# Writing the context part of a cross-attention and FFN kernel out tile by tile, with its side loads in pieces

## The chip, the cores and the metric

The kernel runs on one core of a Trainium2 chip. The metric is the device time of one execution in microseconds (us). Three runs of the kernel before took 1319.31 to 1321.22 us, median 1320.01.

## The reference

The inputs are x (64 x 512 x 512), a context (64 x 77 x 512) and the weights of one attention layer and one FFN layer, all float32. Cut to what matters:

```python
qh = rope(einsum('bse,ehd->bshd', layernorm(x), Wq))   # 16 query heads, 4 key/value heads, 32 wide
kh = rope(einsum('bse,ehd->bshd', ctx, Wk)); vh = einsum('bse,ehd->bshd', ctx, Wv)
attn = softmax(qh @ kh^T / sqrt(32))
x = x + mean_over_heads(attn @ vh) @ Wo
w_scale = mean(abs(weight))
q_weight = sign(weight) * (abs(weight) > 0.5 * w_scale)          # ternary weight
i_scale = max(abs(layernorm(x))) / 127
x = x + (clip(round(layernorm(x) / i_scale)) @ q_weight^T) * w_scale * i_scale + bias
```

## The kernel before, in words

There are three parts. The **context part** turns the 64 x 77 = 4928 context rows into keys and values and writes them to two scratch tensors in HBM, `k_scr` and `v_scr`. Then the attention part goes over 128 pairs of x tiles in a pipeline of seven stages, and last the FFN part goes over the 64 batches. The change touches the context part and the SyncE instructions right behind it; it lies in about the first 120 of 1318 us.

The context part works in 39 tiles of 128 rows (the last has 64), numbered 0 to 38. No scheduler decides anything: each engine has its own instruction list, written by hand, and semaphores join them. Five engines work on a tile:

- SyncE issues nearly all DMAs, in the order of its list. For tile j it loads the context rows of tile j+4 (`ctx_load`, L324) into one of four buffers, stores the keys of tile j-2 and the values of tile j (`kv_store`, L330 and L331; in the last tiles L365 and L371). Each store waits for the data, and what stands behind it on SyncE waits with it.
- TensorE multiplies tile j (`ctx_kv`, L1065, 12 matmuls), transposes the rows of tile j+2 (`ctx_T`, L1054), which waits for the load of that tile, and transposes the keys of tile j-2 (`ctx_kT`, L1073).
- ScalarE copies the transposed rows (L572), the keys and values out of PSUM (L582, L585) and the transposed keys (L595).
- VectorE makes the low parts of the transposed rows for tile j+1 (L753), two small steps on the values of tile j (L776, L781), and the low part of the keys of tile j-2 (L787). Behind these four it does weight preparation in some tiles.
- GpSimd does the rotary embedding of the keys (L478, L484).

The first tiles and the last are written out; the ones between run in a hardware loop of four tiles a turn (on GpSimd two). The weight preparation on VectorE stands in these places: the sum of the four query groups of Wq in tiles 5 to 7 (L801 to L805), the sum of absolute FFN weights in tile 8 (L809), the bias rows in tiles 9 to 12 (L813 to L829), the centring of Wq and the thresholds at tile 32 (L850 to L857), and the ternary FFN weight in tiles 33 to 36, three instructions a tile (L860 to L864). The Wq weight, the FFN weight and the first x batch are loaded with 1 MB each behind tiles 0, 2 and 3 (L344, L347, L351), the second and third x batch near the end (L362), the fourth behind the first keys. The two rotary tables `kcos` and `ksin` (624 KB each) are loaded before the first tile. The first keys and values of the attention part come back from scratch (`kv_step`, L400 and L404, ten DMAs a batch) when all stores have landed.

Of the kernel before, what the change touches and what calls it, by code (L numbers as in the profile page):

```python
# [90 lines left out]
def build(nc, x, ctx_in, wq, wk, wv, wo, fw, fb, ident_d, qcos_d, qsin_d, kcos_d, ksin_d, out):  # L91
# [11 lines left out]
    with stack:  # L103
# [204 lines left out]
        def _(sp):  # L308
            sp.dma_start(ctx_sb[:, 0, :], ctx_rows[0:P, :]).then_inc(c_in[0], 16)
            sp.dma_start(ident[:, :], ident_d).then_inc(ident_in, 16)  # L310
            sp.dma_start(wkv[:, :, 0, :], wk.rearrange("(c p) n -> p c n", p=P)).then_inc(wkv_in, 16)
            sp.dma_start(wkv[:, :, 1, :], wv.rearrange("(c p) n -> p c n", p=P)).then_inc(wkv_in, 16)
            sp.dma_start(ctx_sb[:, 1, :], ctx_rows[P:2 * P, :]).then_inc(c_in[1], 16)
            for n in range(4):
                sp.dma_start(wo4[D * n:D * n + D, :], wo).then_inc(wo_in, 16)
            for n in range(2, 4):
                sp.dma_start(ctx_sb[:, n, :], ctx_rows[P * n:P * n + P, :]).then_inc(c_in[n], 16)
            sp.dma_start(kcos, kcos_d).then_inc(ktable_in, 16)
            sp.dma_start(ksin, ksin_d).then_inc(ktable_in, 16)
# [13 lines left out]

            sp.wait_ge(zeroed, ZEROED)
            for n in range(4):
                ctx_load(n, n)
                if n < 2:
                    sp.wait_ge(v_copied, n + 1)
                    sp.wait_ge(v_ready, n + 1)
                    sp.dma_start(v_scr[n * P:n * P + P, :, :], v_sb[:, n, :, :]).then_inc(v_out[n], 16)  # L340
                else:
                    kv_store(n, n)
                if n == 0:
                    sp.dma_start(wq_sb.rearrange("p c h g d -> p c (h g d)"),  # L344
                                 wq.rearrange("(c p) h g d -> p c (h g d)", p=P)).then_inc(wq_in, 16)
                elif n == 2:
                    sp.dma_start(fw_sb, fw.rearrange("(c p) k -> p c k", p=P)).then_inc(fw_in, 16)  # L347
                    sp.dma_start(qcos[:, :, :], qcos_d).then_inc(qtable_in, 16)
                    sp.dma_start(qsin[:, :, :], qsin_d).then_inc(qtable_in, 16)
                    sp.dma_start(fbias, fb.unsqueeze(0).broadcast_to([BR, E])).then_inc(fb_in, 16)  # L350
            sp.dma_start(x_sb[:, 0, :, :], xv[0]).then_inc(x_in[0], 16)  # L351
            groups = (CT - 4) // 4
            with sp.Fori(1, groups) as g:
                for n in range(4):
                    ctx_load(g * 4 + n, n)
                    kv_store(g * 4 + n, n)
            for j in range(groups * 4, CT + 3):
# [951 lines left out]
```

## Time and profile before

| what | value |
|---|---|
| profiled execution, its span | 1319.5 us, 1317.7 us |
| TensorE matmul, weight load busy | 1267.9 us (96%), 1085.9 us (82%) |
| VectorE, ScalarE, GpSimd busy | 1181.8 us (90%), 1025.1 us (78%), 791.2 us (60%) |
| mean granted TensorE clock | 0.990 of full speed |
| DMA of a context tile | rows in 256 KB, keys out 128 KB, values out 68 KB |
| Wq load, 1024 KB, issued at 15.16 us | 5.7 us to landing |
| `kcos` and `ksin` loads, 624 KB each | 6.1 and 7.1 us to landing |
| main chain of waits, whole execution | VectorE 47%, TensorE 31%, issue 15% |

How to read it: the shares of busy time are averages over all three parts and say little about the context part, which is a tenth of the span. The timeline, cut to one engine, shows each group of instructions with its start, its length and, in brackets, how long the engine was idle before it and what ended that. Times below count from the start of the span. Buffers that lie in the large x and x1 arrays, such as the context rows, the keys and values before they are stored and the FFN weight, all appear under the name `x_sb` in the trace.

### The profile page before, as it was taken

Reading aid. Unit: us, or ns where it says so; the run is one execution under the profiler, and the core shown is the slowest. Engines: PE = TensorE matmul, PEld = TensorE weight load, DVE = VectorE, ACT = ScalarE, POOL = GpSimd, SP = SyncE. Lnnn points to the kernel's source line nnn. Section 1 sums busy time; section 2 is a strip of 40 time slices with the busy share of each in tenths; the row PEclk is TensorE's granted clock in tenths of the full one; section 3 lists DMA queues with packets and bytes.
Section 4 is the critical chain, followed back from the end, with each engine's and each line's share of the span. In section 5 each row is a group of like instructions: output and inputs, shape, how many; then the busy total and the mean of one; then the engine's idle time right before and its main releaser. Section 6 shows DMA issues by size and latency. Waiting matters only on the chain.

```text
span 1317.7 us, 36811 instructions
## 1 busy us (share of the span) xinstructions
PE 1267.9 (96%) x9848; PEld 1085.9 (82%) x9911; DVE 1181.8 (90%) x2772; ACT 1025.1 (78%) x2338; POOL 791.2 (60%) x1536
## 2 busy tenths in 40 slices
PE   5897999999999999999999999999969999999998
PEld 5796999999999999999999999999935555555554
DVE  4876899999999999999999999999978888888887
ACT  3454788888888888888888888888857878888886
POOL 3564888888888888888888888888820000000000
PEclk9999999999999999999999999999979999999999
DMA  8574355555555555555546452323108999999945
GB/s 266 166 216 133 107 158 182 154 183 161 176 165 171 165 171 167 170 171 166 178 159 187 150 169 76 102 80 98 37 5 332 400 401 395 401 399 404 406 201 223
DMA packets 100815, 265.18 MB, mean 201 GB/s; under 512 B 49705, under 2 KB 65769, under 8 KB 72114
## 3 DMA queue, kind: packets, MB, share of 16 engines
q1 hardware_dynamic: 100786, 264.86, 58.8%
q8 instruction: 10, 0.16, 0.1%
q14 instruction: 19, 0.16, 0.0%
HBM read 139.64 MB, written 125.17 MB: 201 GB/s over the span
## 4 chain that ended last, share of the span: by engine, by line
DVE 47%; PE 31%; issue 15%; DMA 2%; DVEq 2%; SPq 1%; ACT 1%; POOL 1%; POOLq 0%; ACTq 0%
PE bank L1248 18%; DVE amax L898 10%; DVE x_sb L930 8%; DVE e_sb L944 6%; DVE mx_sb L940 5%; DVE bn_sb L889 5%; PE bank L1239 4%; PE bank L1246 3%; DVE qT_sb L912 2%; PE bank L1065 2%; DVE rinv_sb L886 2%; DVE ve_sb L918 2%; DVE bn_sb L881 2%; DVE mv_sb L904 1%; DMA x_sb<-in_ctx 1%
## 5 line engine op out<-in xcount | busy, mean ns | idle before, releaser
L1248 PE MATMUL bank<-wT,x_sb 128*128 128x512 f16 x1024 | 263.9, 380 | 3.5 <-issue 0.2
L1168 PE MATMUL bank<-wqs,xT_sb 128*128 128x128 f32 x2048 | 259.7, 280 | 0.2
L718 ACT ACTIVATE x_sb<-bank,mean,cols 128x512 f32<-128x512 f32 x256 | 196.0, 774 | 67.6 <-PE bank L1248 67.3
L1168 PEld LDWEIGHTS bank<-wqs,xT_sb 128*128 128x128 f32 x2048 | 238.2, 191 | 7.1 <-ACT xT_sb L640 0.8
L1216 PE MATMUL bank<-v_blk,pT_sb 103*128 103x136 f32 x1536 | 199.0, 279 | 0.3 <-ACT pT_sb L682 0.3
L1216 PEld LDWEIGHTS bank<-v_blk,pT_sb 103*128 103x128 f32 x1536 | 190.6, 190 | 0.5 <-ACT pT_sb L682 0.5
L1248 PEld LDWEIGHTS bank<-wT,x_sb 128*128 128x128 f16 x1024 | 100.5, 98 | 106.8 <-issue 1.6
L930 DVE SCALAR_TENSOR_TENSOR x_sb<-x_sb,negm,bank 128x512 f32 (+1 forms) x256 | 179.5, 742 | 7.9 <-PE bank L1179 2.7
L898 DVE TENSOR_REDUCE amax<-x_sb (+1 forms) x128 | 156.0, 1218 | 23.2 <-DVE bn_sb L889 8.0
L691 ACT ACTIVATE sq_sb<-x_sb 128x512 bf16 (+1 forms) x256 | 161.4, 631 | 18.7 <-DVE x_sb L930 1.4
L1005 DVE TENSOR_TENSOR x_sb<-x_sb 128x512 f32 (+1 forms) x256 | 164.5, 683 | 1.2 <-ACT x_sb L718 1.2
L682 ACT ACTIVATE pT_sb<-bank 103x384 f32<-103x384 f32 x256 | 111.7, 489 | 53.1 <-PE bank L1189 53.1
L640 ACT ACTIVATE xT_sb<-bank 128x512 f32<-128x512 f32 x256 | 138.9, 595 | 7.6 <-PE bank L1138 3.0
L1203 PE MATMUL bank<-k_blk,qT_sb 128*128 128x308 f32 x768 | 140.1, 317 | 1.8 <-DMA k_blk<-k_scr 1.8
L504 POOL TENSOR_TENSOR rs<-ve_sb,mhalf 128x2 f32 (+1 forms) x128 | 89.5, 700 | 79.9 <-DVE ve_sb L875 79.9
L1138 PE MATMUL bank<-ident,x_sb 128*128 128x128 f32 x1024 | 133.0, 273 | 0.0
L667 ACT ACTIVATE e_sb<-e_sb,rs_sb 128x308 f32<-128x308 f32 x256 | 129.2, 568 | 0.0
L997 DVE TENSOR_SCALAR x_sb<-bank 128x1024 f16<-128x1024 f16 x128 | 88.5, 691 | 44.6 <-PE bank L1239 43.0
L940 DVE TENSOR_REDUCE mx_sb<-bank 128x4 f32<-128x308 f32 x256 | 110.1, 471 | 11.0 <-PE bank L1203 8.1
L1138 PEld LDWEIGHTS bank<-ident,x_sb 128*128 128x128 f32 x1024 | 117.0, 141 | 0.0
L1203 PEld LDWEIGHTS bank<-k_blk,qT_sb 128*128 128x128 f32 x768 | 111.0, 189 | 2.2 <-DMA k_blk<-k_scr 2.0
L1189 PEld LDWEIGHTS bank<-ident,e_sb 128*103 128x103 f32 x768 | 98.5, 168 | 15.4 <-issue 1.3
(126 smaller groups left out, 2584.4 us busy)
## 6 DMA issues: line engine op xcount, KB each, us to landing
out_y<-x_sb SPq DMA_DIRECT2D x112, 1024.0 KB, 7.2
x_sb<-in_x SPq DMA_DIRECT2D x64, 1024.0 KB, 6.5
x_sb<-out_y SPq DMA_DIRECT2D x48, 1024.0 KB, 9.0
x_sb<-in_ctx SPq DMA_DIRECT2D x38, 256.0 KB, 2.8
k_blk<-k_scr SPq DMA_DIRECT2D x256, 19.2 KB, 5.5
k_scr<-x_sb SPq DMA_DIRECT2D x38, 128.0 KB, 2.3
v_scr<-x_sb SPq DMA_DIRECT2D x38, 68.0 KB, 2.3
v_blk<-v_scr SPq DMA_DIRECT2D x128, 10.2 KB
```

Of the source, the lines that this page charges most:

```text
L640: act.activation(xT_sb[:, t, :, :].rearrange("p c r -> p (c r)"), bank[t][:, :], ACT.Copy).then_inc(xT_copied_t, 1)
L691: act.activation(sq_sb[:, :], x1_at(kj, gj, t), ACT.Square, accum_out=ssq[:, bass.ds(2 * j + t, 1)]).then_inc(sq_done, 1)
L718: act.activation(u_sb[:, t, :], bank[4 + t][:, :], ACT.Identity, bias=stat_of(mean1, j, t, back), scale=cols[:, 6:7]).then_inc(scaled_t, 1)
L898: dve.tensor_reduce(amax[:, bass.ds(2 * j, 2)], x1_at(kj, gj).rearrange("p (t e) -> p t e", t=2), AX.X, ALU.max, apply_absolute_value=True ...
L930: dve.scalar_tensor_tensor(out=x1_at(kj, gj, t), in0=x_sb[:, kj // 2, 2 * (kj % 2) + t, :], scalar=negm[:, kj, t:t + 1], in1=bank[t][:, :] ...
L940: dve.tensor_reduce(mx_sb[:, t, :], bank[4 + t][:, 0:SC].rearrange("p (h a) -> p h a", h=HEADS), AX.X, ALU.max).then_inc(mx_ready, 1)
L1005: dve.tensor_tensor(x1_tile, x1_tile, u_sb[:, t, :], ALU.add).then_inc(sum_done_t, 1)
L1138: last = pe.transpose(bank[t][:, c * P:(c + 1) * P], x_sb[:, kj // 2, 2 * (kj % 2) + t, c * P:(c + 1) * P], ident[:, :])
L1168: last = pe.matmul(bank[2][:, t * HD:(t + 1) * HD], xT_sb[:, t, c, :], wqs[:, c, :], start=c == 0, stop=c == EC - 1)
L1203: last = pe.matmul(bank[4 + t][:, 0:SC], qT_sb[:, a, t * P:(t + 1) * P], k_blk[:, slot, b, :].bitcast(F32R), start=n == 0, stop=n == 2)
L1216: last = pe.matmul(bank[6][:, t * HEADS * VC:(t + 1) * HEADS * VC], pT_sb[0:CR, t, c * P:(c + 1) * P], v_blk[0:CR, slot, c, :, :].rearrang ...
L1248: last = pe.matmul(bank[4 + t][:, :], q16T_sb[:, t, c, :], wT[:, c, :], start=False, stop=c == EC - 1)
```

## The change

The hardware loops of the context part are gone on all engines: its 39 tiles are written out, and the side work is placed by tile number. The 1 MB loads of Wq and the FFN weight become four pieces of 256 KB each, behind tiles 3 to 6 and 8 to 11; the rotary tables come as their first 8 tiles' rows ahead and the rest (496 KB each) behind tiles 1 and 2; the four x batches are loaded behind tiles 16, 22, 28 and 34. The keys and values of batches 0 and 1 are fetched behind tiles 20 and 30 instead of after all stores. The loads of Wk, Wv and Wo are issued by ScalarE instead of SyncE. On VectorE the Wq sum moves to tiles 9 to 11, the absolute sum is cut into four (tiles 13 to 16), the Wq centring stands in tile 16, the bias rows in 17 to 20, the thresholds in 21, and the ternary weight takes tiles 22 to 33, one instruction each. SyncE's order in a tile is context load, key store, value store, and then the side load. The core of the diff:

```diff
+KFIRST = 8
+WQ_SUM, WQ_MEAN, WQ_CENTRE = 9, 14, 16
+FW_SUM, FW_MEAN, FW_CUT, FW_TERN = 13, 19, 21, 22
+BIAS_ROWS = 17
+FW_T = FW_TERN + 4
+KV_AHEAD = (20, 30)
...
-            groups = (CT - 4) // 4
-            with sp.Fori(1, groups) as g:
-                for n in range(4):
-                    ctx_load(g * 4 + n, n)
-                    kv_store(g * 4 + n, n)
...
+            for j in range(CT + 3):
+                if j + 4 <= CT:
+                    sp.wait_ge(cT_done, j + 1)
+                    sp.dma_start(ctx_sb[0:rows, j % 4, :], ctx_rows[(j + 4) * P:(j + 4) * P + rows, :])\
...
+                if j == 1:
+                    sp.dma_start(kcos[:, KFIRST:CT + 1, :], kcos_d[:, KFIRST:CT + 1, :]).then_inc(ktable_in, 16)
+                elif j == 2:
+                    sp.dma_start(ksin[:, KFIRST:CT + 1, :], ksin_d[:, KFIRST:CT + 1, :]).then_inc(ktable_in, 16)
+                elif 3 <= j < 3 + EC:
+                    sp.dma_start(wq_sb[:, j - 3, :, :, :].rearrange("p h g d -> p (h g d)"), wq_rows[:, j - 3, :])\
+                      .then_inc(wq_in, 16)
+                elif 8 <= j < 8 + EC:
+                    sp.dma_start(fw_sb[:, j - 8, :], fw_rows[:, j - 8, :]).then_inc(fw_in, 16)
+                elif j == 12:
+                    sp.dma_start(fbias, fb.unsqueeze(0).broadcast_to([BR, E])).then_inc(fb_in, 16)
+                    sp.dma_start(qcos[:, :, :], qcos_d).then_inc(qtable_in, 16)
+                    sp.dma_start(qsin[:, :, :], qsin_d).then_inc(qtable_in, 16)
+                elif j in (16, 22, 28, 34):
+                    x_load((j - 16) // 6)
+                elif j in KV_AHEAD:
+                    b = KV_AHEAD.index(j)
...
+                    kv_step(b, b)
...
-            kv_step(0, 0)
-            kv_step(1, 1)
-            batch_step(3, 3, 0, store=False)
...
+            act.dma_start(wkv[:, :, 0, :], wk.rearrange("(c p) n -> p c n", p=P)).then_inc(wkv_in, 16)
+            act.dma_start(wkv[:, :, 1, :], wv.rearrange("(c p) n -> p c n", p=P)).then_inc(wkv_in, 16)
+            for n in range(4):
+                act.dma_start(wo4[D * n:D * n + D, :], wo).then_inc(wo_in, 16)
...
+                if FW_SUM <= j < FW_SUM + EC:
+                    c = j - FW_SUM
+                    dve.wait_ge(fw_in, 16 * EC)
+                    then(dve.tensor_reduce(fsum4[:, c:c + 1], fw_sb[:, c, :], AX.X, ALU.add,
+                                           apply_absolute_value=True))
...
+                o, part = (j - FW_TERN) // 3, (j - FW_TERN) % 3
+                if 0 <= o < EC:
+                    if part == 0:
+                        then(dve.tensor_scalar(fpos[:, o, :], fw_sb[:, o, :], cols[:, 2:3], None, ALU.is_gt))
+                    elif part == 1:
+                        then(dve.tensor_scalar(fneg[:, o, :], fw_sb[:, o, :], cols[:, 3:4], None, ALU.is_lt))
+                    else:
+                        dve.tensor_tensor(w16[:, o, :], fpos[:, o, :], fneg[:, o, :], ALU.subtract).then_inc(f_tern, 1)
```

SyncE's list in the loop of the kernel before, two tiles of a turn and its end (`x_sb<-in_ctx` is a context load, ISA and REGISTER_ALU rows compute and wait):

```order
L324 DMA x_sb<-in_ctx 128x512
L330 ISA
L330 DMA v_scr<-x_sb 128x136
L331 REGISTER_ALU
L331 DMA k_scr<-x_sb 256x1x128
L324 ISA
L324 DMA x_sb<-in_ctx 128x512
L330 ISA
L330 DMA v_scr<-x_sb 128x136
L331 REGISTER_ALU
L331 DMA k_scr<-x_sb 256x1x128
L353 REGISTER_ALU
```

SyncE's list in the changed kernel around tile 20 (line numbers of the changed kernel):

```order
L343 DMA x_sb<-in_ctx 128x512
L348 DMA k_scr<-x_sb 256x1x128
L354 DMA v_scr<-x_sb 128x136
L328 DMA k_blk<-k_scr 32x2x77 x4
L332 DMA v_blk<-v_scr 77x34
L332 DMA v_blk<-v_scr 26x34
L332 DMA v_blk<-v_scr 51x34
L332 DMA v_blk<-v_scr 52x34
L332 DMA v_blk<-v_scr 25x34
L332 DMA v_blk<-v_scr 77x34
L343 DMA x_sb<-in_ctx 128x512
```

Before, only stores stood between two context loads; now ten loads of keys and values stand between the stores of tile 20 and the next context load.

VectorE's list in the kernel before, tile 33, where the ternary weight is made:

```order
L753 TENSOR_TENSOR cT_parts<-bank,cT_parts 128x512
L776 TENSOR_TENSOR x_sb<-x_sb,wbar 128x128
L781 TENSOR_REDUCE x_sb<-x_sb 128x4
L787 TENSOR_TENSOR x_sb<-bank,x_sb 128x128
L860 TENSOR_SCALAR x_sb<-x_sb,cols 128x512
L863 TENSOR_SCALAR x_sb<-x_sb,cols 128x512
L864 TENSOR_TENSOR x_sb<-x_sb 128x512
L753 TENSOR_TENSOR cT_parts<-bank,cT_parts 128x512
```

VectorE's list in the changed kernel, tiles 22 and 23 (L734 is the old L753, L830 and L832 the old L860 and L863):

```order
L734 TENSOR_TENSOR cT_parts<-bank,cT_parts 128x512
L757 TENSOR_TENSOR x_sb<-x_sb,wbar 128x128
L762 TENSOR_REDUCE x_sb<-x_sb 128x4
L768 TENSOR_TENSOR x_sb<-bank,x_sb 128x128
L830 TENSOR_SCALAR x_sb<-x_sb,cols 128x512
L734 TENSOR_TENSOR cT_parts<-bank,cT_parts 128x512
L757 TENSOR_TENSOR x_sb<-x_sb,wbar 128x128
L762 TENSOR_REDUCE x_sb<-x_sb 128x4
L768 TENSOR_TENSOR x_sb<-bank,x_sb 128x128
L832 TENSOR_SCALAR x_sb<-x_sb,cols 128x512
```

The three instructions of one quarter of the weight, which stood together in one tile, now stand in three tiles, one in each.

## Rows read from the trace of the kernel before

**Rows 1.** Busy us of each engine by stretch (x instructions), TensorE clock, DMA.
```profile
28.00:29.00 1.00, 0.00 (x0) 0.00 (x0) 0.00 (x0) 0.00 (x0) 0.00 (x0) 0.57 1.09 397
...
58.00:80.00 22.00, 21.21 (x172) 19.87 (x170) 16.00 (x41) 12.47 (x40) 14.03 (x31) 1.00 0.74 210
```

**Rows 2.** TensorE timeline, starts of tiles 1, 9, 10, 14, 15, 20, 31, 38.
```profile
14.28 1.77 PE L1065 MATMUL bank<-wkv_parts,cT_parts 128*128 128x256 f32 x12
...
39.70 1.70 PE L1065 MATMUL bank<-wkv_parts,cT_parts 128*128 128x256 f32 x12
...
43.36 1.70 PE L1065 MATMUL bank<-wkv_parts,cT_parts 128*128 128x256 f32 x12 [1.41 <-DVE cT_parts L753]
...
54.52 1.70 PE L1065 MATMUL bank<-wkv_parts,cT_parts 128*128 128x256 f32 x12 [0.86 <-DVE cT_parts L753]
...
56.52 1.67 PE L1065 MATMUL bank<-wkv_parts,cT_parts 128*128 128x256 f32 x12
...
67.76 1.70 PE L1065 MATMUL bank<-wkv_parts,cT_parts 128*128 128x256 f32 x12
...
91.53 1.68 PE L1065 MATMUL bank<-wkv_parts,cT_parts 128*128 128x256 f32 x12
...
111.91 1.57 PE L1065 MATMUL bank<-wkv_parts,cT_parts 128*64 128x256 f32 x12 [0.86 <-DVE cT_parts L753]
```

**Rows 3.** TensorE timeline, context transposes that waited, and two tiles.
```profile
21.52 0.66 PE L1054 MATMUL bank<-ident,x_sb 128*128 128x128 f32 x4 [1.63 <-DMA x_sb<-in_ctx]
...
29.95 1.11 PE L1054 MATMUL bank<-ident,x_sb 128*128 128x128 f32 x4 [4.25 <-DMA x_sb<-in_ctx]
...
30.92 2.91 PE L1065 MATMUL bank<-wkv_parts,cT_parts 128*128 128x256 f32 x12
...
34.63 1.83 PE L1065 MATMUL bank<-wkv_parts,cT_parts 128*128 128x256 f32 x12
...
91.00 0.66 PE L1054 MATMUL bank<-ident,x_sb 128*128 128x128 f32 x4
```

**Rows 4.** SyncE timeline: DMA issues.
```profile
15.64 0.50 SPq L324 DMA_DIRECT2D x_sb<-in_ctx  x1
...
88.18 0.35 SPq L324 DMA_DIRECT2D x_sb<-in_ctx  x1
...
99.63 0.43 SPq L362 DMA_DIRECT2D x_sb<-in_x  x1
...
120.45 2.61 SPq L400 DMA_DIRECT2D k_blk<-k_scr  x4
...
123.10 2.29 SPq L404 DMA_DIRECT2D v_blk<-v_scr  x6
```

**Rows 5.** Landing times of line 324 (context rows) and line 362 (x).
```profile
DMA to landing us min/median/max: 2.6/2.8/7.8
...
DMA to landing us min/median/max: 5.7/5.8/5.8
```

**Rows 6.** VectorE timeline: weight preparation, and one tile with no extra work.
```profile
35.61 0.94 DVE L803 TENSOR_TENSOR wqs<-wqs,x_sb 128x512 f32<-128x512 f32 x1
...
98.08 0.69 DVE L851 TENSOR_TENSOR wqs<-wqs,x_sb 128x512 f32<-128x512 f32 x1
...
99.12 0.69 DVE L753 TENSOR_TENSOR cT_parts<-bank,cT_parts 128x512 fp32r<-128x512 f32 x1
...
100.56 0.48 DVE L860 TENSOR_SCALAR x_sb<-x_sb,cols 128x512 f32<-128x512 f32 x1
```

**Rows 7.** Timeline of all engines where the context part hands over.
```profile
114.56 0.59 ACT L619 ACTIVATE wT<-bank 128x512 f16<-128x512 f16 x1
...
124.79 1.12 PE L1203 MATMUL bank<-k_blk,qT_sb 128*128 128x308 f32 x6 [1.78 <-DMA k_blk<-k_scr]
...
125.05 0.74 POOL L554 TENSOR_TENSOR qa_sb<-qa_sb,qb_sb 128x256 f32<-128x256 f32 x1
...
126.62 0.38 PE L1150 MATMUL bank<-ident,qa_sb 128*128 128x128 f32 x2
```

More of the change, by code:

```diff
@@ L206, in build @@
         fpos = early(EC, E)
+        fsum4 = early(EC)
         w16 = early(EC, E // 2).bitcast(F16)
@@ new lines, in x_load, with kv_step @@
+            def x_load(b):
+                sp.dma_start(x_sb[:, b, :, :], xv[b]).then_inc(x_in[b], 16)
+            def kv_step(b, k):
+                at_least(sp, sc_done_t, 4 * (b - 2) + 4)
+                for h in range(HEADS):
+                    sp.dma_start(k_blk[D * h:D * h + D, k % 2, :, CTX * h:CTX * h + CTX],
+                                 k_scr[D * h:D * h + D, :, bass.ds(b * CTX, CTX)]).then_inc(k_in[k % 2], 16)
+                at_least(sp, pv_done, 2 * (b - 2) + 2)
+                for c, r, n, h, a in SEGS:
+                    sp.dma_start(v_blk[r:r + n, k % 2, c, h, :], v_scr[bass.ds(b * CTX + a, n), h, :])\
+                      .then_inc(v_in[k % 2], 16)
@@ L372, in _ @@
                       .then_inc(v_out[j % 4], 16)
+                if j == 1:
[15 more added lines that the diff above has]
+                    b = KV_AHEAD.index(j)
+                    for m in range(2):
+                        sp.wait_ge(k_out[m], 16)
+                        sp.wait_ge(v_out[m], 16)
+                    kv_step(b, b)
             sp.wait_ge(k_out[0], 16 * (CT // 2 + 1))
@@ L488, in _ @@
             pool.wait_ge(ktable_in, 32)
-            ctx_step(0, 0)
-            ctx_step(1, 1)
-            with pool.Fori(1, CT // 2) as g:
-                for n in range(2):
-                    ctx_step(g * 2 + n, n)
-            for j in range(2 * (CT // 2), CT + 1):
+            for j in range(CT + 1):
+                if j == KFIRST:
+                    pool.wait_ge(ktable_in, 64)
                 ctx_step(j, j % 2, P if j < CT else CLAST)
@@ L791, in _ @@
             wq_sum = wqs[:, :, :].rearrange("p c (h d) -> p (c h) d", h=HEADS)
-            for j in range(CHEAD):
-                if j >= 1:
-                    low_ctx(j + 1, (j + 1) % 2)
-                ctx_step(j, j % 4, j // 4)
-                if j >= 2:
+            for j in range(CT + 3):
+                if 1 <= j < CT:
+                    low_ctx(j + 1, (j + 1) % 2, P if j + 1 < CT else CLAST)
+                if j <= CT:
+                    ctx_step(j, j % 4, j // 4, P if j < CT else CLAST)
+                if 0 <= j - 2 < CT:
@@ L1077, in _ @@
             ctx_T(1, 1, 0)
-            for j in range(4):
+            for j in range(CT + 3):
                 if j == 0:
```

184 lines of the change are left out of this document (51 added, 133 removed).

## The prediction

> **What bounds the kernel now.** I read the busy time by stretch first. The change lies in the context part, which ends near 118 us. Everything behind it is the same instructions in the same order, so a gain or loss in the context part reaches the end of the kernel at full size. While 22 us of the old loop run, TensorE is busy 21.21 of them, VectorE 16.00, and the DMA engines' share is 0.74 at 210 GB/s [rows 1]. So the part is close to TensorE's pace where nothing disturbs it, but only just.
>
> Second, the timeline of TensorE. Call "step n" the time from the start of tile n's key and value matmuls (L1065) to the next tile's. Step 14 took 54.52 to 56.52: 2.00 us, TensorE never idle. The starts of steps 1, 9, 15, 20, 31 and 38 are 14.28, 39.70, 56.52, 67.76, 91.53 and 111.91 [rows 2]. That makes five stretches: A (8 steps) 25.42 us, B (6) 16.82, C (5) 11.24, D (11) 23.77, E (7) 20.38. At 2.00 a step they would need 74.0 of their 97.6 us. Three things make up the difference.
>
> (1) In A, TensorE waits for context rows: 1.63 us before 21.52 and 4.25 us before 29.95. Behind the second wait the clock is down: transposes take 1.11 us where 0.66 is usual, and step 6 takes 3.71 us (30.92 to 34.63) [rows 3]; the granted clock was 0.57 in 28 to 29 us, on its way to the 1.2 GHz level, with TensorE idle since 25.7 [rows 1]. Cold work cost 3.71-2.00, and 0.5 on the transposes: 2.2 us.
>
> (2) In B and E, VectorE's weight preparation stands between tiles. Its own four instructions a tile take 1.44 us (99.12 to 100.56) [rows 6], so 0.56 us a step are free. Step 9, with the 2048-wide absolute sum, took 3.66 us; steps 10 to 13 with the bias rows took 11.16 [rows 2].
>
> (3) In the loop the context load comes just in time: issued at 88.18, transposes of that tile at 91.00, as it lands (median landing 2.8) [rows 3, 4, 5]. SyncE issues it behind the two stores of an earlier tile, so its lead over the transposes is three steps minus the key/value chain. I put the slack at 0.2 us, an estimate: it is 0 in this row, a load issued just behind the loop's branch, and the whole loop loses only 0.16 a step against 2.00 (D, below), so the three loads of a turn without the branch before them have little more or less than their due. Anything issued ahead of a context load beyond that is TensorE idle time.
>
> **The change, part by part.** A base step in straight-line code: I take 2.05, between step 14's 2.00 and D's mean of 23.77/11 = 2.16.
>
> *Head loads in pieces (A).* The 1 MB loads of Wq, the FFN weight and x leave A; two table rests of 496 KB and four 256 KB pieces come in. At 397 GB/s [rows 1] 496 KB take 1.25 us, and one more issue costs 0.43 (99.63) [rows 4]. Ahead of a context load that is 0.43 + (1.25-0.43) - 0.2 = 1.05 late. A lateness in consecutive steps is paid once for two steps, because a step made longer gives the next load its lead; early loads also have about 0.3 more. Tables: 0.8. Pieces: 0.43 + 0.2 - 0.2 = 0.4 to 0.45, four of them, paid twice: 0.9. A = 16.4+0.8+0.9 = 18.1: **-7.3**. From both sides: -8 (no lateness) to -3 (a wait like the 1.63 and a cold restart stay).
>
> The skill page "DMA: Bandwidth & Descriptors" (Trainium skill, section Bandwidth) speaks against pieces: batch to 1 MiB or more. Here a 256 KB context load lands in 2.8 us and a 1 MB x load in 5.8, so by that rule four pieces one behind the other would hold the queue 4 x 2.8 - 5.8 = 5.4 us longer per weight, and A would gain 2 instead of 7. I don't take it: nothing waits between pieces, so their fixed part overlaps.
>
> *Weight and Wo loads issued by ScalarE.* They still land before the first matmuls, which hang on a chain of conversions behind them. I take 0; bounds: one issue earlier each, -0.9, to ScalarE being later, +0.4. The Trainium skill (same page, section Issuing engines are not separate DMA queues) says issuing from several engines saves only issue time; by it this is 0 to -0.9. No run here shows it.
>
> *FFN and Wq pieces and sums (B).* Four FFN pieces (2 x 0.45) overlap the three Wq sums, each up to 0.94 us (35.61) [rows 6] against 0.56 free: together 1.1. The absolute sum becomes four quarters of the one that cost step 9 1.6 us; they fit in the free 0.56 but for 0.1 each. The Wq mean's eight matmuls now stand in step 14: 0.9. B = 12.3+1.1+0.1+0.9 = 14.4: **-2.4**. The bias rows leave B for C and D.
>
> *C.* Three small loads behind tile 12: 3 x 0.43, of which step 14's 0.9 covers most: 0.4. Step 16 has the last quarter, its sum and the Wq centring (0.69 at 98.08 and its factor) [rows 6]: 1.2 over. First bias step 0.44, quarters 0.3. The x load behind tile 16 stands ahead of a context load. A context load issued at 15.64, right behind the 1 MB of Wq, was waited for until 21.52 [rows 3, 4]: 5.9 us, 3.1 more than 2.8. Late by 3.1+0.43-0.2 = 3.3, less the 1.4 by which steps 17 and 18 are longer: 2.0; I take 1.3, since an x load has 8 KB rows and 1 MB at 397 GB/s is 2.6 us. C = 10.25+1.2+0.44+0.3+0.4+1.3 = 13.9: **+2.7**.
>
> *D.* The other bias steps [rows 2]: 11.16 - 4 x 2.05 = 2.96, less what fell in C and under the x stall: 1.83. Transposes of the FFN weight, two groups at 0.25 each (an estimate; four small f16 transposes each): 0.5. The ternary steps, one instruction a tile, fit in 0.56 free. Then the early keys: behind tile 20 SyncE issues four key and six value loads, 2.61+2.29 = 4.9 us [rows 4], while the next context load and all stores wait behind it. Late by 4.9-0.2, less 1.1 of longer steps: 3.6 us idle in step 23. That is nearer to the 4.25 that let the clock fall than to the 1.63 that didn't: +2.2. The x load behind tile 22 comes within two steps of it and finds its lateness paid by the stall and the cold work. D = 22.55+1.83+0.5+3.6+2.2 = 30.7: **+6.9**.
>
> *E.* Before, the ternary work made a step 2.9 us (20.38/7; less VectorE's own 1.44 it is 1.5 a tile). Now 14.35 + 0.5 transposes. The x load behind tile 28 hits step 31 and the ten key loads behind tile 30 hit step 33; the second finds the first's stall in its lead, so both together cost about 4.9-0.2 = 4.65 (2 to 7 with a cold clock). E = 19.5: **-0.9**.
>
> *The seam.* The first score matmuls waited 1.78 us for the first keys (124.79) [rows 7]; those lie there now. But the next transposes (126.62) need GpSimd's result, which ends at 125.79, so 0.8 of it is gained. The last ternary copy on ScalarE (0.59 at 114.56) and its wait no longer stand before the x transposes' copies: 1.0. Together **-1.8** (0 to -3). The fourth x load leaves SyncE there: nothing waits for it.
>
> **Sum.** -7.3-2.4+2.7+6.9-0.9-1.8 = -2.8 us. The profiled execution took 1319.5, so 1316.7; the median of the runs shown lies 0.5 above it: 1317.
>
> **The rivals.**
> - *The lead is long enough.* If context loads have several us of lead in straight-line code (no register work on SyncE), no stall appears: -1.3-3.6-2.2-4.65, so 1305. For it: the loop's own steps of 2.00 beside a 0.74 DMA share. Against it: the wait ends with the landing itself in the loop, and two steps without one don't make 5 us.
> - *The DMA queue is full* (the other side: slower). Place: the context load behind each x load in steps 16, 22, 28. The longest landing of a context load was 7.8 us [rows 5], not 5.9, when stores and big loads were mixed. Then each of the three is 1.9 later: +2.6 at 16 (with the full 2.0), +2.7 at 22, +2.9 at 28 with a cold clock: 1317+8.2 = 1325. It decides from a landing of about 6.5 us. For it: 0.74 share leaves a quarter of the engines, and four more MB go through in 18 steps. Against it: the in_x loads beside the last tiles landed in 5.7 to 5.8 [rows 5].
> - *The pieces don't clear the head.* If A keeps one wait and a cold restart (3.8 us), 1321: no change that can be told. For it: a piece of 256 KB comes on top of a tile's 256+128+68 KB. Against it: these 708 KB in 2 us are about 360 GB/s, under the 397 seen.
>
> **How the numbers follow.** Chances: my sum 0.5 (its own range 1313 to 1321), lead long enough 0.15, queue full 0.25, head not cleared 0.1. A measurement of this kernel tells 0.2%, 2.6 us, from no change. My sum lies on that border: half of it faster, 0.26, nearly all the rest same. Faster 0.26+0.15 = 0.41; same 0.22+0.08+0.04 = 0.34; slower 0.21+0.04 = 0.25. Range 1307 to 1326: it leaves out most of the first rival and the upper end of the second.
>
> **What would show it.** Step 9 should start near 32 us, step 15 near 47, step 20 near 61, step 31 near 91 to 92, step 38 near 111. TensorE's waits at the context transposes should be one of 3 to 4 us for tile 25, and one or two for tiles 33 and 35, with a granted clock below 1 behind the first; the first score matmuls should wait for no keys. If step 38 starts before 104, the lead was longer than I read; if tiles 21 and 27 wait over 2 us each, the queue was full.

## The result, and the profile after

Times are in us. A ratio is a kernel's time over that of the kernel before, run beside it on the same chip, with its 95% interval.

The changed kernel took **1326.72** (median of 4 runs, 1325.88 to 1327.07), the kernel before 1320.62 (4 runs, 1319.31 to 1322.25): ratio **1.0053 [1.0035, 1.0070]**, slower by about 6, where 1317 was forecast. The kernels below were timed on several chips, each beside the kernel before, so they are compared by their ratios. The profiled execution has a span of 1323.8, against 1317.7. The starts of steps 1, 9, 15, 20, 31 and 38 on TensorE are 13.26, 32.79, 49.14, 63.62, 95.95 and 115.15 now, and the first score matmuls start at 129.95. That gives, term by term:

| stretch | before | forecast | after |
|---|---|---|---|
| start to step 1 | 14.28 | 14.28 | 13.26 |
| A, steps 1 to 8 | 25.42 | 18.1 | 19.53 |
| B, 9 to 14 | 16.82 | 14.4 | 16.35 |
| C, 15 to 19 | 11.24 | 13.9 | 14.48 |
| D, 20 to 30 | 23.77 | 30.7 | 32.33 |
| E, 31 to 37 | 20.38 | 19.5 | 19.20 |
| seam, step 38 to the first score matmuls | 12.88 | 11.1 | 14.80 |
| the rest of the span | 1192.91 | 1192.9 | 1193.85 |

Against the forecast, 8.9 are lost: 3.7 in the seam, 1.4 + 1.9 + 0.6 + 1.6 in A, B, C and D, 0.9 behind the seam, less 1.0 won at the start and 0.3 in E.

TensorE's waits between 12 and 135 us (idle us in total, times, longest; before, the context rows cost 6.3 in 3 waits, two of them in [rows 3]):

```profile
PE bank L1024 <- DMA x_sb<-in_ctx: 14.4, 12, 2.9
PE bank L1035 <- DVE cT_parts L734: 3.2, 5, 1.1
PE bank L1111 <- POOL qa_sb L541: 2.2, 2, 1.1
PE bank L1043 <- DVE x_sb L768: 1.5, 1, 1.5
PE bank L1129 <- ACT xT_sb L621: 1.4, 1, 1.4
```

TensorE no longer waits 1.63 and 4.25, with a cold clock behind the second, as in [rows 3], but twelve times for shorter. (Cold means at the lower of the clock's two levels, 1.2 GHz, or on the way to it.) Busy time, granted clock and DMA share of the stretches that answer to [rows 1], and of the seam:

```profile
28.00:29.00 1.00, 1.00 (x11) 1.00 (x10) 0.58 (x2) 0.60 (x3) 0.34 (x1) 1.00 0.88 328
58.00:80.00 22.00, 15.91 (x116) 14.80 (x115) 15.61 (x39) 7.50 (x26) 8.31 (x18) 0.92 0.66 200
95.00:113.00 18.00, 14.88 (x112) 13.93 (x109) 12.35 (x30) 8.37 (x26) 8.29 (x18) 0.91 0.72 211
120.00:130.00 10.00, 7.53 (x43) 7.13 (x43) 4.11 (x15) 3.44 (x8) 2.80 (x4) 0.66 0.17 46
```

At 28 us the clock is whole now (0.57 before). From 58 to 80 TensorE is busy 15.9 of 22 where it was 21.2, and in the seam the granted clock is 0.66. The early key and value loads on SyncE, which answer to 120.45 and 123.10 in [rows 4]:

```profile
68.32 2.62 SPq L328 DMA_DIRECT2D k_blk<-k_scr  x4
70.97 2.27 SPq L332 DMA_DIRECT2D v_blk<-v_scr  x6
73.29 0.37 SPq L343 DMA_DIRECT2D x_sb<-in_ctx  x1
```

What stands behind them is the context load of tile 25, at 73.29. Its rows on TensorE:

```profile
76.11 1.11 PE L1024 MATMUL bank<-ident,x_sb 128*128 128x128 f32 x4 [2.94 <-DMA x_sb<-in_ctx]
77.02 0.42 PE L1043 MATMUL bank<-ident,x_sb 128*128 128x128 f32 x1
77.09 2.67 PE L1035 MATMUL bank<-wkv_parts,cT_parts 128*128 128x256 f32 x12
```

That is the wait forecast for tile 25 (3.6 forecast, 2.94 measured), with cold work behind it (1.11 for 0.60, 2.67 for 1.67). The context loads that stand right behind the x loads of tiles 16, 22 and 28 on SyncE, and the transposes of their rows (tiles 21, 27 and 33) on TensorE:

```profile
56.53 0.43 SPq L343 DMA_DIRECT2D x_sb<-in_ctx  x1
77.32 0.44 SPq L343 DMA_DIRECT2D x_sb<-in_ctx  x1
93.62 0.45 SPq L343 DMA_DIRECT2D x_sb<-in_ctx  x1
```

```profile
62.88 0.66 PE L1024 MATMUL bank<-ident,x_sb 128*128 128x128 f32 x4 [1.73 <-DMA x_sb<-in_ctx]
83.13 0.66 PE L1024 MATMUL bank<-ident,x_sb 128*128 128x128 f32 x4 [1.40 <-DMA x_sb<-in_ctx]
99.48 0.86 PE L1024 MATMUL bank<-ident,x_sb 128*128 128x128 f32 x4 [1.87 <-DMA x_sb<-in_ctx]
```

From issue to transposes it is 6.35, 5.81 and 5.86. The seam is what was not forecast. SyncE first, then ScalarE, then TensorE:

```profile
111.50 0.45 SPq L322 DMA_DIRECT2D x_sb<-in_x  x1
112.45 0.57 SPq L348 DMA_DIRECT2D k_scr<-x_sb  x1
```

```profile
117.64 0.28 ACT L586 ACTIVATE x_sb<-bank 128x128 fp32r<-128x128 f32 x1 [1.89 <-DMA k_scr<-x_sb]
...
120.53 0.28 ACT L586 ACTIVATE x_sb<-bank 128x128 fp32r<-128x128 f32 x1 [2.02 <-DMA k_scr<-x_sb]
120.71 1.08 ACT L621 ACTIVATE xT_sb<-bank 128x512 f32<-128x512 f32 x2
122.80 0.23 ACT L586 ACTIVATE x_sb<-bank 128x64 fp32r<-128x64 f32 x1 [1.01 <-DMA k_scr<-x_sb]
```

```profile
121.35 3.78 PE L1129 MATMUL bank<-wqs,xT_sb 128*128 128x128 f32 x16 [1.36 <-ACT xT_sb L621]
...
129.95 1.10 PE L1164 MATMUL bank<-k_blk,qT_sb 128*128 128x308 f32 x6
```

The fourth x load (111.50) goes out just ahead of a key store (112.45). That store lands 5.11 later, by the chain of waits:

```profile
112.45 5.11 DMA k_scr<-x_sb
118.27 2.18 DMA k_scr<-x_sb
```

ScalarE may not overwrite one of the **two** key buffers until its store has landed, so it stands for 1.89, 2.02 and 1.01. The copies of the x transposes stand behind that on ScalarE, TensorE is idle, and its first query matmuls take 3.78 cold, 2.05 before. The granted clock fell to 0.50, the 1.2 GHz level, from 121 to 127. The score matmuls have no wait for keys (1.78 in [rows 7]), but they start later all the same.

### The profile page after: what moved, and what is told of

It is laid out like the page before. It is cut to its first block, busy times and chain, and to the rows that moved or that the text cites. A ratio compares the mean times of both kernels' runs of the same rounds, so it can differ in the third digit from the quotient of the medians.

```text
span 1323.8 us, 36413 instructions
## 1 busy us (share of the span) xinstructions
PE 1274.9 (96%) x9911; PEld 1089.9 (82%) x9911; DVE 1183.5 (89%) x2776; ACT 1025.9 (77%) x2338; POOL 791.2 (60%) x1536
## 4 chain that ended last, share of the span: by engine, by line
PE 87%; DVE 4%; DMA 3%; issue 1%; SPq 1%; POOL 1%; ACT 1%; DVEq 0%; POOLq 0%; ACTq 0%
PE bank L1129 17%; PE bank L1209 17%; PE bank L1177 13%; PE bank L1099 8%; PE bank L1164 8%; PE bank L1150 6%; PE bank L1200 4%; PE bank L1140 4%; PE bank L1207 4%; DMA x_sb<-in_ctx 2%; PE bank L1111 2%; PE bank L1119 2%; PE bank L1035 2%; DMA k_scr<-x_sb 1%; PE bank L1024 1%
```

## The experiments

Stretches of one profiled execution of each of eleven kernels (seam as above):

| kernel | start | A | B | C | D | E | seam | span |
|---|---|---|---|---|---|---|---|---|
| after | 13.26 | 19.53 | 16.35 | 14.48 | 32.33 | 19.20 | 14.80 | 1323.8 |
| x4_late | 14.18 | 20.84 | 18.69 | 14.00 | 34.09 | 18.81 | 11.67 | 1324.6 |
| keys_late | 12.83 | 19.15 | 19.53 | 16.72 | 31.74 | 19.03 | 15.91 | 1328.9 |
| kv_spread | 13.54 | 19.99 | 16.78 | 14.02 | 30.13 | 18.13 | 14.32 | 1321.1 |
| old_side | 12.68 | 20.70 | 17.52 | 14.44 | 27.50 | 17.95 | 17.64 | 1322.2 |
| lead2 | 14.10 | 21.36 | 16.30 | 13.13 | 34.13 | 19.59 | 15.32 | 1327.6 |
| k4 | 14.35 | 20.79 | 16.99 | 14.29 | 33.94 | 20.84 | 10.71 | 1325.5 |
| lead2_k4 | 13.94 | 15.80 | 18.35 | 13.13 | 28.73 | 15.60 | 12.97 | 1311.1 |
| roomy_keys_late | 13.20 | 17.01 | 18.26 | 13.12 | 27.28 | 15.60 | 12.47 | 1309.8 |
| roomy_old_side | 13.23 | 15.81 | 18.69 | 13.22 | 27.30 | 15.60 | 14.40 | 1312.4 |
| before_roomy | 13.96 | 19.79 | 16.97 | 10.24 | 22.96 | 20.27 | 12.08 | 1309.4 |

One stretch of one execution moves by 1 to 2 with nothing done to it (compare A of the first five), so single stretches are read only for larger differences.

### One part of the change undone at a time

**x4_late**: the fourth x load behind all stores.

```diff
-                elif j in (16, 22, 28, 34):
+                elif j in (16, 22, 28):
...
+            x_load(3)
             kv_step(2, 2)
```

> The changed kernel, with the fourth x load issued behind all stores instead of behind tile 34. Theory (this load fills the DMA queues ahead of the last key stores; ScalarE's copy of later keys into the same buffer waits for their landing, TensorE idles and its clock falls at the hand-over): ScalarE's waits for k_scr stores drop from 4.9 us to under 3, the clock stays full between 120 and 127 us, the time from the last tile's matmuls to the first score matmuls falls from 14.8 us to 11 to 12, the whole by 3 to 4 us, ratio to before 1.002 to 1.003. Rival (the early key loads and late stores alone make that hand-over long): 14.8 stays within 0.5 us and the ratio stays 1.005. My prediction's step said nothing waits for this load.

Measured: 1326.80 (1321.3 to 1328.35, 6 runs), 1.0054 [1.0037, 1.0072]. The seam is 3.1 shorter and runs at full clock (120 to 127 us, of this kernel and then of after):

```profile
120.00:127.00 7.00, 5.41 (x45) 4.79 (x44) 3.87 (x11) 2.47 (x9) 3.17 (x7) 1.00 0.30 84
```

```profile
120.00:127.00 7.00, 5.49 (x24) 5.09 (x24) 3.54 (x12) 2.58 (x7) 1.30 (x2) 0.52 0.25 66
```

In the seam ScalarE's waits for key stores are down to 1.72 and 1.43 (4.9 in three after). So the seam's mechanism is shown by the trace, and k4, below, shows it from the other side: with the load in its place and four key buffers the seam is 10.71. The time as a whole didn't fall: A, B and D of this execution were longer by 5.4, one of its waits for a key store is 4.01 in D (so 7.2 in all, where under 3 was expected), and the intervals can't tell 3 from nothing. The gain was given back or drowned; this run doesn't say which.

**keys_late**: no early keys and values.

```diff
-KV_AHEAD = (20, 30)
+KV_AHEAD = ()
...
+            kv_step(0, 0)
+            kv_step(1, 1)
```

> The changed kernel, with the first two batches of keys and values fetched behind all stores, as before the change. Theory (ten key loads on SyncE delay the next context load by their issue time of 4.9 us): the waits of the context transposes of tiles 25 and 35 (2.94 us with a cold restart, 0.96) vanish, stretch D from 32.3 us to 28, E shorter by 0 to 1, and the hand-over gains 1 to 2 us of waiting for keys: whole 3 to 4 us less than the changed kernel, ratio 1.002 to 1.003. Rival (the DMA engines are the limit, not SyncE's issue): the waits move to other tiles, D stays above 31 us, ratio 1.005 to 1.006.

Measured: 1325.07 (1321.11 to 1331.71, 9 runs), 1.0047 [1.0030, 1.0064]. The waits at tiles 25 and 35 are gone, but those at tile 16 and, behind the x loads, at 21, 27 and 33 are 2.7, 2.6, 2.3 and 2.2 (0.6, 1.7, 1.4 and 1.9 after), and D is shorter by 0.6 only: the rival's case, with other waits in place of the two. The profiled execution was one of the slowest of the nine (1330.89, 5.8 over the median), so these sizes are those of a bad execution.

**kv_spread**: the twenty key and value loads of batches 0 and 1 one a tile, from tile 17, instead of ten at a time.

```diff
-KV_AHEAD = (20, 30)
+KV_AHEAD = (17, 30)
...
+                if KV_AHEAD[0] <= j < KV_AHEAD[0] + 20:
+                    b, i = (j - KV_AHEAD[0]) // 10, (j - KV_AHEAD[0]) % 10
...                    # one of kv_step's ten loads
```

> The changed kernel, with the twenty key and value loads of the first two batches one behind each of tiles 17 to 36 instead of ten behind tile 20 and ten behind tile 30. Theory (SyncE's issue time in one block of 4.9 us makes tile 25's wait of 2.9 us and the cold restart behind it): that wait goes, the clock stays full between 72 and 80 us, each tile gets 0.3 to 0.6 us later instead; stretch D 29 to 31 us instead of 32.3, whole 1 to 3 us less: ratio 1.003 to 1.0045. Rival (total issue time of SyncE counts, however it is cut): D and E together stay at 51.5 us within 1, ratio 1.005.

Measured: 1324.69 (1323.66 to 1330.20, 6 runs), 1.0043 [1.0026, 1.0060]. The cold restart at tile 25 is gone, D and E are 2.2 and 1.1 shorter, as expected, but the context waits still add up to 12.1, and ScalarE's waits for key stores to 12.5 (4.9 after). The ratio is 0.0010 below the changed kernel's; the intervals overlap.

**old_side**: all later transfers at their old places.

```diff
-                elif j in (16, 22, 28, 34):
-                    x_load((j - 16) // 6)
+                elif j in (16, CT - 5, CT - 2):
+                    x_load((16, CT - 5, CT - 2).index(j))
...
+            kv_step(0, 0)
+            kv_step(1, 1)
+            x_load(3)
```

> The changed kernel, with the x and key loads where they stood before the change, but for the first x load (behind tile 16): second and third x load behind tiles 33 and 36, the fourth and the first keys behind all stores. Writing out, pieces and the spread weight preparation stay. Theory (what the change gives in the head and in the ternary tiles is real, and the x and key loads between tiles 20 and 34 take it back through waits of context rows and key stores, with cold restarts): stretch D falls from 32.3 us to 24.5 to 26, tile 38 starts at 105 to 108, ratio to before 0.996 to 0.998. Rival (the written-out part is slower by itself): D stays above 29, ratio 1.003 or more.

Measured: 1322.52 (1320.37 to 1325.72, 11 runs), 1.0021 [1.0012, 1.0031]. D falls from 32.33 to 27.50; the seam is the longest of all, with an x load (tile 36) ahead of the last key stores. More than half of the loss goes with the places of the transfers, but D stays 3.7 above before, so they are not all.

**weights_sync**: Wk, Wv and Wo issued by SyncE again.

```diff
-            act.dma_start(wkv[:, :, 0, :], ...)
+                    sp.dma_start(wkv[:, :, 0, :], ...)      # Wv and Wo likewise
```

> The changed kernel, with the loads of Wk, Wv and Wo back on SyncE, in the order context 0, Wk, Wv, context 1, Wo. Theory (ScalarE's issuing brought the first matmuls forward by 1.0 us: 10.12 to 9.10): first key and value matmuls at 10.0 to 10.4 us, the whole 0.5 to 1 us slower, ratio 1.0055 to 1.006. Rival (the early context 1 load and the short tables did it, or the gain is taken back by later waits for context rows): first matmuls later but tile 9 within 0.3 us of 32.8, no change of the whole.

Measured: 1328.95 (1327.35 to 1330.94, 6 runs), 1.0074 [1.0062, 1.0086]. The first matmuls start at 9.56 (9.10 after), step 1 at 13.72 (13.26), step 9 at 34.50 (32.79). By the medians ScalarE as issuer is worth some 2 us, but the intervals overlap, and kernels with the head of after start step 1 at 12.68 (old_side) to 14.35 (k4): a gain is not shown.

**side_act**: tables, Wq, FFN weight and x loads issued by ScalarE, so that nothing large stands ahead of a context load on SyncE's list.

```diff
-                    sp.dma_start(kcos[:, KFIRST:CT + 1, :], ...)
+                    act.dma_start(kcos[:, KFIRST:CT + 1, :], ...)     # the others likewise
```

> The changed kernel, with the side loads (table rests, Wq and FFN weight pieces, the four x loads) issued by ScalarE behind its work on the same tile, so that they lie in another queue than context loads and stores; order and sizes are the same. Theory A (what costs is standing behind a big load in the same queue): packets of both queues interleave, median landing of context loads falls from 3.5 to about 3, the 1.7 to 2.1 us waits of tiles 7, 21 and 33 fall under 1, whole 3 to 5 us less than the changed kernel: ratio 1.001 to 1.003. Theory B (bandwidth while a big load runs, whatever the queue): landing and waits as before within 0.5 us, ratio 1.005 or more.

Measured: 1329.07 (1326.90 to 1332.13, 6 runs), 1.0067 [1.0053, 1.0080]. TensorE waits 15.0 for context rows (14.4 after), which land in 3.8 (median; 3.7 after). So it doesn't matter which engine issues the big loads; what is left is their traffic itself, which the runs here moved but never took away. The Trainium skill ("DMA: Bandwidth & Descriptors", section Issuing engines are not separate DMA queues) says that another issuing engine saves issue time only; this run agrees.

### Room instead of places

**lead2**: each context load two tiles earlier, as soon as its buffer is free.

```diff
+LEAD = 2
...
-                if j + 4 <= CT:
-                    rows = P if j + 4 < CT else CLAST
-                    sp.wait_ge(cT_done, j + 1)
-                    sp.dma_start(ctx_sb[0:rows, j % 4, :], ctx_rows[(j + 4) * P:(j + 4) * P + rows, :])\
...
+                for m in (range(LEAD + 1) if j == 0 else (j + LEAD,)):
+                    if m + 4 <= CT:
+                        rows = P if m + 4 < CT else CLAST
+                        sp.wait_ge(cT_done, m + 1)
+                        sp.dma_start(ctx_sb[0:rows, m % 4, :], ctx_rows[(m + 4) * P:(m + 4) * P + rows, :])\
...
```

> The changed kernel, with each context load issued two tiles earlier on SyncE (the four buffers allow it). Theory (context loads have no slack in SyncE's order, and every side load ahead of one shows as TensorE idle time): the 15.3 us or so of waits for context rows behind the first matmuls fall under 2 us, tile 38 starts at about 103 instead of 115.15, the hand-over is as long as in the changed kernel or a little longer; ratio 0.995 to 0.998. Rival (the DMA engines are full and the queue sets the pace): waits fall by less than half, tile 38 starts after 109, ratio above 1.000.

Measured: 1326.74 (1325.52 to 1330.01, 6 runs), 1.0060 [1.0047, 1.0073]. Every context wait behind the first matmuls is gone, and not a microsecond is won. That refuted my theory, that these waits alone are the loss. ScalarE's waits for key stores in this kernel, 12 to 135 us, then one place of them on ScalarE and on TensorE:

```profile
ACT x_sb L588 <- DMA k_scr<-x_sb: 24.8, 14, 4.7
```

```profile
86.72 0.28 ACT L588 ACTIVATE x_sb<-bank 128x128 fp32r<-128x128 f32 x1 [4.68 <-DMA k_scr<-x_sb]
86.89 0.59 ACT L565 ACTIVATE cT_parts<-bank 128x512 fp32r<-128x512 f32 x1
```

```profile
88.58 2.18 PE L1037 MATMUL bank<-wkv_parts,cT_parts 128*128 128x256 f32 x12 [4.18 <-DVE cT_parts L736]
90.56 1.06 PE L1026 MATMUL bank<-ident,x_sb 128*128 128x128 f32 x4
```

ScalarE stands 4.68 for a key buffer; the copy of the context transposes is next in its list, VectorE makes the low part from that copy, and TensorE waits for VectorE. The trace names VectorE at TensorE's wait; one has to go two engines back to find the store. This **second path** was 4.9 in after, hidden behind the first.

**k4**: four key buffers instead of two, nothing else.

```diff
-        kT_sb = early(2, 2, P)
+        kT_sb = early(4, 2, P)
...
-                at_least(act, k_out[m], 16 * g)
+                at_least(act, k_out[j % 4], 16 * (j // 4))
```

> The changed kernel with four key buffers and nothing else. Theory (two buffers' paths stand side by side: context rows and key stores; each alone gives nothing, as the earlier context loads alone showed): ScalarE's waits for key stores go from 4.9 us to under 1, TensorE's waits for context rows stay at 13 to 17 us, the hand-over after the last tile shrinks from 14.8 to about 12: ratio 1.002 to 1.005. Rival (key stores were the main cost and the waits for context rows follow from them): waits for context rows fall under 8 us, ratio under 1.000.

Measured: 1326.37 (1322.62 to 1327.48, 6 runs), 1.0044 [1.0030, 1.0058]. The mirror image: waits for key stores 0.8, for context rows 17.7. The seam falls to 10.71, with the clock full from 121 to 132 us; the time doesn't fall.

**lead2_k4**: both edits.

> The changed kernel, with context loads issued two tiles earlier and with four instead of two buffers for the transposed keys that are stored. Theory A (the 24.8 us for which ScalarE waits for key stores to land, in the kernel with the context loads earlier alone, took the place of the waits for context rows; both stand behind the same big loads in SyncE's queue): with room for both, ScalarE's waits for key stores fall under 3 us, tile 38 starts at 102 to 106 us, ratio to before 0.993 to 0.997. Theory B (the DMA engines' whole capacity sets the pace): waits come back at a third place (value stores or context rows), tile 38 after 112, ratio above 1.002.

Measured: **1313.30** (1312.46 to 1314.85, 5 runs), **0.9952 [0.9939, 0.9966]**. 0 and 0 make 13. TensorE and ScalarE (12 to 135 us):

```profile
PE bank L1036 <- DVE cT_parts L735: 10.7, 15, 2.0
PE bank L1025 <- DMA x_sb<-in_ctx: 0.2, 1, 0.2
```

```profile
ACT x_sb L587 <- DMA k_scr<-x_sb: 2.7, 2, 2.0
```

A, D and E are 3.7, 3.6 and 3.6 shorter than after. What TensorE waits for now is VectorE.

**lead2_k4_act**: the same with side_act's issues.

> Context loads two tiles earlier, four key buffers, and the side loads issued by ScalarE. If a load in another queue also helps the key stores and the context rows (theory A of the two kernels that do these alone), this is the fastest: tile 38 at 100 to 104 us, ratio 0.991 to 0.996. If buffers and lead already give all the room there is, it equals the kernel with those two within 0.1%, or is up to 0.1% slower by ScalarE's issue time (0.45 us in 14 tiles, of which ScalarE's idle time hides most).

Measured: 1315.41 (1307.96 to 1317.72, 10 runs), 0.9958 [0.9942, 0.9974]: no difference that can be told.

**roomy_x4_sums**: lead2_k4 with x4_late, and the Wq and FFN sums one tile later (`WQ_SUM = 10`, `FW_SUM = 14`), since VectorE waited for both weights.

> Context loads two tiles earlier and four key buffers, and on top the fourth x load behind all stores and the Wq and FFN sums each one tile later. In the kernel without these two VectorE waited 1.7 us for Wq and 2.1 us for the FFN weight, and from the last tile's matmuls to the first score matmuls it took 13.0 us where 11.7 were seen without the fourth x load. If these waits are on the path, they come off: 2 to 4 us less, ratio 0.992 to 0.994. If the pipeline around them absorbs them, the ratio stays at 0.995.

Measured: 1312.84 (1312.01 to 1314.40, 5 runs), 0.9949 [0.9936, 0.9962]: as lead2_k4. B fell to 15.16 and C rose to 15.49; the wait only changed its place.

**roomy_keys_late**: lead2_k4 with keys_late.

> Context loads two tiles earlier and four key buffers, with the first keys fetched behind all stores as before the change. Asks what the early key loads are worth once nothing waits for SyncE's issue: if they bring the 0.8 us that I counted for the hand-over or up to 2, this kernel is that much slower than the one with early keys (0.9952): ratio 0.996 to 0.9965. If their 9.8 us of issue on SyncE still cost in D and E, it is faster: 0.993 or less.

Measured: **1312.43** (1310.40 to 1314.64, 6 runs), **0.9944 [0.9930, 0.9957]**. With room, early keys are worth nothing: the score matmuls wait 1.6 for them, and that wait is bought back in D (27.28 for 28.73).

### What is the change itself worth?

**before_roomy**: the kernel before, 1 MB head loads and all, with the same two edits (SyncE's part written out for them; the other engines keep their loops).

```diff
-                    ctx_load(g * 4 + n, n)
+                    ctx_load(g * 4 + (n + LEAD), (n + LEAD) % 4)
...
-        kT_sb = early(2, 2, P)
+        kT_sb = early(4, 2, P)
```

> The kernel before, hardware loops and 1 MB head loads and all, with the two kinds of room alone: context rows loaded two tiles earlier, four key buffers instead of two (SyncE's own loop is written out for it; every other engine keeps its loop). Theory A (the change has a value of its own, about 4 to 8 us of spread weight preparation and head pieces, which the two tight paths hid): this kernel gains only its own waits, 6.3 us of context waits and about 2 us of cold clock less what stays behind the 1 MB loads, so 1313 to 1317, 2 to 5 us above the changed kernel with the same room (1312.4 to 1313.3). Theory B (the change is worth nothing by itself; all of the 13 us came from the room): this kernel is at 1312 or less, and its stretches B and E, where the weight preparation stands, are no longer than with the change by more than what the context waits gave.

Measured: **1311.38** (1311.17 to 1313.65, 5 runs), **0.9943 [0.9928, 0.9958]**. Theory B's time came: the kernel before with room is as fast as any version of the changed one, within the intervals, about 2 us either way. Its second sign did not: E is 4.7 longer than in roomy_keys_late, and C and D make that up (below). Two things stay open here: SyncE's written-out list is itself a part of the change, and no run gives this kernel one kind of room alone. TensorE and ScalarE, 12 to 135 us:

```profile
PE bank L1070 <- DVE cT_parts L758: 8.4, 11, 1.6
PE bank L1059 <- DMA x_sb<-in_ctx: 2.3, 2, 1.3
```

```profile
ACT x_sb L588 <- DMA v_scr<-x_sb: 2.0, 2, 1.1
```

**roomy_old_side**: roomy_keys_late with old_side's x loads.

> The changed kernel with two tiles of lead, four key buffers, no early keys, and the x loads at their old places (tiles 16, 33, 36 and the fourth behind all stores). Theory A (with room the transfers' places don't matter): as with x loads at 16, 22, 28, 34: 1312.4, within 1.5. Theory B (the traffic beside D costs DMA time even so): D shorter than 27.28, near 24 to 25, and the time 1309 to 1311; but the x loads at 33 and 36 then stand ahead of the last key stores and may give 1 to 3 us of it back in the seam.

Measured: 1314.42 (1313.58 to 1315.42, 5 runs), 0.9961 [0.9946, 0.9975]. Theory A for D: 27.30 against 27.28 with the x loads in its midst. The whole is 2.0 above roomy_keys_late, a little outside theory A's 1.5, and the seam, 14.40 for 12.47, is 1.9 of that. So D's last 3.5 (over before) to 4.3 (over before_roomy) are not the x loads. VectorE of this kernel in D (start, length), then one instruction of GpSimd:

```profile
77.19 0.48 DVE L834 TENSOR_SCALAR x_sb<-x_sb,cols 128x512 f32<-128x512 f32 x1
77.71 0.69 DVE L738 TENSOR_TENSOR cT_parts<-bank,cT_parts 128x512 fp32r<-128x512 f32 x1
78.55 0.47 DVE L761 TENSOR_TENSOR x_sb<-x_sb,wbar 128x128 f32<-128x128 f32 x1
79.13 0.29 DVE L766 TENSOR_REDUCE x_sb<-x_sb 128x4 f32<-128x128 f32 x1
79.33 0.28 DVE L772 TENSOR_TENSOR x_sb<-bank,x_sb 128x128 fp32r<-128x128 f32 x1
79.53 0.71 DVE L836 TENSOR_SCALAR x_sb<-x_sb,cols 128x512 f32<-128x512 f32 x1
80.28 0.69 DVE L738 TENSOR_TENSOR cT_parts<-bank,cT_parts 128x512 fp32r<-128x512 f32 x1
...
81.81 0.94 DVE L838 TENSOR_TENSOR x_sb<-x_sb 128x512 f16<-128x512 f32 x1
82.67 0.68 DVE L738 TENSOR_TENSOR cT_parts<-bank,cT_parts 128x512 fp32r<-128x512 f32 x1
```

```profile
79.49 0.46 POOL L478 TENSOR_TENSOR x_sb<-x_sb 128x128 f32<-128x128 f32 x1
```

VectorE waits for no other engine here, and a tile takes it 2.57 and 2.39 with a ternary instruction in it. Its own four instructions take 1.82 and 1.53, not 1.44 [rows 6], and the ternary ones 0.71 and 0.94. The lengths go with what GpSimd does. Eleven of the twelve ternary instructions of this kernel run for about 0.4 beside GpSimd's addition (L478) and take 0.70 to 0.71 (comparisons) and 0.94 to 0.97 (subtractions); the twelfth, at 77.19, runs while GpSimd is idle and takes 0.48. In before GpSimd is idle during all eight comparisons, which take 0.48 each, and the subtractions take 0.69, two of them beside 0.2 to 0.3 of GpSimd's multiplications. So one instruction a tile falls on GpSimd's work for the keys, three in a row behind VectorE's own four did not. That is read from the traces; no run changes only this.

The ternary instructions and what else the kernel before had packed into tiles 32 to 36 (E) is spread over D now. Given the same room, the changed kernel (roomy_keys_late) against before_roomy is: start -0.8, A -2.8, B +1.3, C +2.9, D +4.3, E -4.7, seam +0.4. The sum of these is +0.7: **the weight preparation was moved, not removed**, and the VectorE time that it fills up was no more free in one place than in the other.

## Why the prediction was wrong, point by point

- **The step that failed: the path that it had wrong in the seam.** "The fourth x load leaves SyncE there: nothing waits for it." It moved to 111.50, ahead of the last six key stores. The prediction followed each moved load only to the next *context load* behind it. Here the late one is a store, the waiter ScalarE, and the price -1.8 forecast, +1.9 measured, and 0.9 more behind it (from the first score matmuls to the query matmuls at 139.28 it is 9.33; the same took 8.33 before). x4_late and k4 showed the mechanism: seam 11.67 and 10.71, at full clock. This is the largest single miss, 3.7 of 8.9 (4.6 with what is behind it); the four stretches below missed 5.6 together. And undoing it alone didn't make the kernel faster (x4_late 1.0054): both paths had to be relieved.
- **A, B, C and D: the right mechanism, too small.** Forecast 77.1 together, measured 82.7. The forecast priced each side load by its own lateness and let the traffic around it be free; context waits of 0.4 to 2.1 stand at tiles 6, 7, 11, 13, 16, 18, 21 and 27 (8.4 in all). At 6 and 7 they are 2.6 (1.7 forecast for A's loads), at 11, 13 and 16 2.3 (0.9 for the FFN pieces), at 21 1.7 (1.3), at 27 1.4 (nothing: "finds its lateness paid"). The median landing of context rows rose from 2.8 to 3.7 (side_act: whoever issues the big loads); the longest, 6.4, is under the 7.8 of before.
- **The rival "the DMA queue is full"** named the result within 2 (1325) and the sign, and that was luck. By its own test, over 2 us at tiles 21 and 27, it wasn't met (1.73 and 1.40), and the context rows behind the x loads were there after 6.35, 5.81 and 5.86: close to the 5.9 of the sum, not the 7.8 of the rival. The loss is spread over more tiles than it said, and the largest single part is the seam, which it didn't name.
- **A's wait and the cold restart.** The large term was right in kind: -7.3 forecast, -5.9 measured, no cold clock at 28 us. That four pieces one behind the other would leave a gain of 2 only, which the prediction set aside, did not show.
- **Tile 25 and 33.** Forecast idle 3.6 with a cold restart; measured 2.94 and 1.87, both with one (2.67 and 2.91 for 1.67).
- **ScalarE as issuer.** Taken at 0, within -0.9 to +0.4. The start came 1.0 earlier in the profiled execution, just outside, but in others with the same head step 1 starts at 14.18 (x4_late) and 14.35 (k4), for 14.28 before. Nothing here speaks clearly against the 0.
- **"The ternary steps, one instruction a tile, fit in 0.56 free."** Wrong: [rows 6] show 0.48 for one, but beside GpSimd's addition they take 0.70 and more (roomy_old_side, 8 of 12 in after). Hidden in the changed kernel, because VectorE catches up while TensorE stands for a DMA. With room the steps of D are 2.48 each on average instead of 2.09 (27.28/11, 22.96/11).
- **Never seen: the second path.** [rows 4, 5] held context and x loads; the landing of the key stores was not read at all. ScalarE's waits for them were 2.7 in before. Two paths, each just in time, hide each other: lead2 alone 0, k4 alone 0, both 13.

Still open: why the time differs by up to 10 between executions of one kernel (keys_late, 1321.11 to 1331.71; lead2_k4_act, 1307.96 to 1317.72), what the traffic of the big loads costs by itself, and what a VectorE instruction would take in D with GpSimd's addition moved away from it.

## What to carry to other kernels

Before spreading side transfers or side work over a pipeline, list every buffer ring that a DMA frees or fills, stores too, and how much each has to spare; when two are tight, relieving one shows nothing, so relieve them together, and only then judge the order. Do that to the old kernel as well: here the room (more lead, more key buffers) was the whole gain as far as the intervals tell, and the rearrangement gave nothing with it and cost 6 us without it. Side work spread "one instruction a tile" is free only if the engine's own work per tile, measured in the densest stretch, really leaves that much, and if it takes no longer where it is put: read its length beside the engines that run there.

## What the runs showed of the hardware

- A store of 128 KB behind a 1 MB load landed after 5.11 (112.45 above); the median of such stores is 3.0 in after and 2.3 in before.
- Moving some 7 MB of side loads (two tables of 0.5, Wq, the FFN weight and four x batches of 1) to another issuing engine's list changed neither the landing (3.8, 3.7) nor the waits (15.0, 14.4).
- With more lead and more buffers the transfers landed later (context rows 3.7 in after, 4.4 in lead2_k4; key stores 3.0 and 4.1), and the kernel was 13 us faster: the later landing cost nothing where there was room for it.
- VectorE's comparison of 128x512 took 0.48 alone and 0.70 to 0.71 with about 0.4 of it beside GpSimd's addition; the subtraction 0.69, and 0.94 to 0.97 (before, roomy_old_side).
- In after the clock went down behind idle times of 2.94 (tile 25) and 1.87 (tile 33), but not behind 2.10 (tile 7), nor behind 2.83 in x4_late (tile 25): the length of the last wait alone doesn't tell; in the seam, behind waits of 1.51 and 1.36 with short transposes between, it fell to 0.50 for 6 us.
